# Second expert product of the last seventeen turns as f16 products, and second weights stored as one run per partition

## The reference, cut to what matters

```python
D, HID, E, TOPK = 192, 768, 8, 2
logits = xn2 @ w_gate
top_vals, top_idx = jax.lax.top_k(logits, TOPK)
gates = jax.nn.softmax(top_vals, axis=-1)
gates_full = zeros((T, E)).at[arange(T)[:, None], top_idx].add(gates)
def body(acc, p):
    w1, bb1, w2, bb2, g = p
    h = jax.nn.gelu(xn2 @ w1 + bb1, approximate=False)
    return (acc + g[:, None] * (h @ w2 + bb2), None)
```

## Time and profile before

| what | value |
|---|---|
| profiled execution | 2601.49 us, span 2599.6 us |
| median of three runs | 2596.96 us |
| busy: PE, PEld, DVE | 2382.5, 1836.3, 1658.9 us |
| busy: ACT, POOL | 1158.6, 1042.2 us |
| PE clock granted, mean | 0.935 of full |
| DMA | 262.98 MB, mean 101 GB/s |

### The profile page before, as it was taken

How to read it: one execution, slowest core, us unless ns; L and a number is a source line. 1 busy time by engine, 2 the same in 40 slices (tenths; PEclk the granted TensorE clock), 3 DMA queues, 4 the chain that set the end, 5 groups by cost and what they waited for, 6 DMA issues and landing times. The chain is left out here.

```text
span 2599.6 us, 64053 instructions
## 1 busy us (share of the span) xinstructions
PE 2382.5 (92%) x19496; PEld 1836.3 (71%) x19496; DVE 1658.9 (64%) x4146; ACT 1158.6 (45%) x2240; POOL 1042.2 (40%) x1196
## 2 busy tenths in 40 slices
PE   5589999999999999999999999999999988999886
PEld 4456666666666666677777777777777667888886
DVE  3558888888888888867767776777667731111111
ACT  2234443444433444355555565555555643333332
POOL 2103333333333333244444444444444454555555
PEclk8679999999999998899999999999999999999998
DMA  7432222321223222544344455544534356878774
GB/s 136 150 40 33 33 34 46 45 32 33 34 41 50 32 32 36 135 91 97 102 110 98 106 114 118 113 96 106 117 89 104 95 158 197 219 209 226 203 214 122
DMA packets 250837, 262.98 MB, mean 101 GB/s; under 512 B 35477, under 2 KB 230489, under 8 KB 250777
## 3 DMA queue, kind: packets, MB, share of 16 engines
q1 hardware_dynamic: 213912, 229.95, 37.2%
q0 software_dynamic: 36864, 32.27, 7.2%
HBM read 212.21 MB, written 52.83 MB: 102 GB/s over the span
## 5 line engine op out<-in xcount | busy, mean ns | idle before, releaser
L1347 DVE TENSOR_REDUCE MX<-PS 108x2 f32<-108x648 f32 x576 | 456.0, 824 | 45.6 <-PE PS L1769 40.9
L1042 ACT ACTIVATE pool<-PS 108x648 f32<-108x648 f32 x576 | 387.4, 714 | 216.5 <-PE PS L1792 186.4
L890 POOL DMA_INDIRECT out<-big,tokn x192 | 304.2, 1584 | 436.2 <-DVE big L1497 232.2
L1648 PE MATMUL PS<-WB,big 128*128 128x192 f32 x2304 | 406.3, 332 | 2.5 <-ACT big L1071 2.5
L1071 ACT ACTIVATE big<-PS,WF 128x256 f32<-128x256 f32 x576 | 242.2, 473 | 371.6 <-PE PS L1648 369.9
L1648 PE MATMUL PS<-XE,WF 128*128 128x256 f16 x2880 | 366.4, 279 | 35.3 <-DMA WF<-w1p 28.2
L1648 PEld LDWEIGHTS PS<-WB,big 128*128 128x128 f32 x2304 | 375.6, 192 | 27.4 <-issue 18.5
L1648 PEld LDWEIGHTS PS<-XE,WF 128*128 128x128 f16 x2880 | 277.9, 100 | 91.2 <-issue 33.5
L867 POOL DMA_INDIRECT xbuf<-XR,DST x192 | 190.5, 992 | 242.5 <-issue 197.8
L1497 DVE SCALAR_TENSOR_TENSOR big<-PS,grow,GB 128x192 f32<-128x192 f32 x192 | 71.3, 413 | 273.5 <-POOL GB L878 144.2
L1803 PE MATMUL PS<-pool,Vp 108*32 108x324 f32 x2304 | 217.5, 520 | 0.0
(11 more groups left out here) (197 smaller groups left out, 4104.1 us busy)
## 6 DMA issues: line engine op xcount, KB each, us to landing
WF<-w1p SPq DMA_DIRECT2D x96, 771.5 KB, 5.1
WB<-in_L_ffn_W SPq DMA_DIRECT2D x96, 576.0 KB, 4.7
ximg<-in_x SPq DMA_DIRECT2D x96, 196.0 KB, 5.3
XtR<-xbuf SPq DMA_DIRECT2D x96, 196.0 KB, 2.5
ximg<-in_x SPq DMA_DIRECT2D x96, 195.1 KB, 8.7
B2t<-in_L_ffn_b SPq DMA_DIRECT2D x96, 96.0 KB, 5.3
out<-R SPq DMA_DIRECT2D x32, 243.0 KB
w1p<-WF SPq DMA_DIRECT2D x8, 768.0 KB, 4.0
```

The costliest lines, as they stand in the source:

```text
L890: nc.gpsimd.indirect_dma_start(rows_out, bass.IndirectOffsetOnAxis(ap=tokn[:, i, s_:s_ + 1], axis=0), Yt[:, i, s_, :], None, bounds_check= ...
L1042: nc.scalar.activation(Pr[:, at:at + 2, :], pair(("st", p))[0:TP, :, 0:T], ACT.Exp, scale=SCALE2).then_inc(S["ex"], 1)
L1347: nc.vector.tensor_reduce(MX[:, qt, g, 64 * jj:64 * jj + 64:32], pair(("s", p))[0:TP, :, 0:T], AX.X, ALU.max).then_inc(S["mx"], 1)
L1648: last = nc.tensor.matmul(out_ap, lhsT, rhs, start=(i == 0), stop=(i == len(products) - 1))
```

## The change

1. **Second weights and bias row in one run.** Two DRAM tensors hold, for each expert and partition, 1152 numbers of second weights and 192 of second bias, 5376 bytes in one run. `w2p` holds float32 and is read in the turns up to 14. `w2h` holds the weights times 64, split into f16 high and low halves, and is read in turns 15 to 31 (loads issued in CLOSE and TILES). One DMA in `load_down` takes the place of two.
2. **Filling them.** Before turn 2, SP writes the bias rows of both. In turns 2 and 3, which are now written out instead of being in the loop, four steps `down` each split one expert's second weights on ACT and DVE (128x1152 per instruction), and SP writes them to `w2h`. After turn 3, SP issues 8 DMAs from DRAM to DRAM that fill `w2p`.
3. **Turns of tiles alone.** Gelu writes back in place into PE's accumulator (`ge_alone`, same instructions and shapes). ACT copies each unit to f16 (`gh`, 128x512), DVE subtracts that from the accumulator and writes the rest as f16 (`gl`, 128x512). The second product is 36 f16 products in place of 12 float32 ones (high by high, high by low, low by high). A bank of `W1` is now free when `gl` is done, and `W2` waits for `gl`. `gm` has one more small instruction (gate divided by 64).

```diff
+W2ROW = NC * D + D
...
+DOWN = {2: (0, 1, 2, 3), 3: (4, 5, 6, 7)}
+ALONE = B + 2 - LAG
...
+ALONE_AHEAD = dict(ACT=("ghi",), DVE=("glo", "gr"))
...
-    ("gm", 0), ("gb", 0), ("lr", 0), ("W1", 0, 0), ("ge", 0, 0), ("X", 1), ("xe", 1), ("gm", 1), ("gb", 1), ("lr", 1),
-    ("W1", 0, 1), ("ge", 0, 1), ("W1", 0, 2), ("ge", 0, 2), ("lu", 0), ("W1", 1, 0), ("ge", 1, 0), ("X", 2),
...
+    ("gm", 0), ("gb", 0), ("lr", 0), ("W1", 0, 0), ("ge", 0, 0), ("gh", 0, 0), ("gl", 0, 0), ("X", 1), ("xe", 1),
+    ("gm", 1), ("gb", 1), ("lr", 1), ("W1", 0, 1), ("ge", 0, 1), ("gh", 0, 1), ("gl", 0, 1), ("W1", 0, 2),
+    ("ge", 0, 2), ("gh", 0, 2), ("gl", 0, 2), ("lu", 0), ("W1", 1, 0), ("ge", 1, 0), ("gh", 1, 0), ("gl", 1, 0),
+    ("X", 2), ("xe", 2), ("W1", 1, 1), ("ge", 1, 1), ("gh", 1, 1), ("gl", 1, 1), ("W2", 0, 0), ("W2", 0, 1),
+    ("yv", 0), ("ld", 0), ("ad", 0), ("gm", 2), ("gb", 2), ("lr", 2), ("W1", 1, 2), ("ge", 1, 2), ("gh", 1, 2),
+    ("gl", 1, 2), ("lu", 1), ("W1", 2, 0), ("ge", 2, 0), ("gh", 2, 0), ("gl", 2, 0), ("X", 0), ("xe", 0),
...
+                out.insert(12 + 40 * j, ("down", k))
...
-    name = FREED[step[0]]
+    name = "glo" if step[0] == "W1" and turn.plan is TILES else FREED[step[0]]
...
+        hid16 = big[:, 0:3 * NC * TILE].bitcast(F16).rearrange("p (r s c t) -> p r s c t", r=3, s=2, c=NC)
...
+        def down_views(k):
+
+            w = WF1[:, k % 3, 0:NC * D].bitcast(F16).rearrange("p (s n) -> p s n", s=2)
+            return WB2[:, k % 2, 0:NC * D], w[:, 0, :], w[:, 1, :]
...
+            def down(k):
+                if k < 2:
+                    sp.wait_ge(att_lo, ATT)
+                    sp.wait_ge(stg_lo, NSTG)
+                else:
+                    sp.wait_ge(down_lo, k - 1)
+                sp.dma_start(WB2[:, k % 2, 0:NC * D].rearrange("p (c n) -> p c n", c=NC),
+                             w2[k].rearrange("(c p) n -> p c n", p=128)).then_inc(down_in[k % 2], 16)
+
+            def down_out(k):
+                sp.wait_ge(down_lo, k + 1)
+                sp.dma_start(w2h[k, :, 0:NC * D], WF1[:, k % 3, 0:NC * D]).then_inc(w2h_out[k % 3], 16)
...
+                w2m = w2h if plan[0] is TILES or plan[0] is CLOSE else w2p
...
-                sp.dma_start(WB2[:, i, :, :], w2[bass.ds(e, 1), :, :].rearrange("a (c p) n -> p (a c) n", p=128)
+                sp.dma_start(WB2[:, i, :], w2m[bass.ds(e, 1), :, :].rearrange("a p n -> (a p) n")
                              ).then_inc(S[f"down{i}"], 16)
-                sp.dma_start(B2t[:, i, :], b2[bass.ds(e, 1), :].to_broadcast([128, D])).then_inc(S[f"down{i}"], 16)
...
+            for w in (w2p, w2h):
+                sp.dma_start(w[:, :, NC * D:].rearrange("e p n -> p e n"),
+                             b2.rearrange("(a e) n -> a e n", a=1).to_broadcast([128, E, D])).then_inc(b2_out, 16)
+            for k in range(2):
+                down(k)
+            for b in DOWN:
+                run(Turn(ATTEND, b, b - 1, b - 2, None))
+            for e in range(E):
+                sp.dma_start(w2p[e, :, 0:NC * D].rearrange("p (c n) -> p c n", c=NC), w2[e].rearrange("(c p) n -> p c n", p=128)
+                             ).then_inc(w2_out, 16)
...
+            def down(k):
+                v, hi, lo = down_views(k)
+                act.wait_ge(down_in[k % 2], 16 * (k // 2 + 1))
+                if k < 3:
+                    act.wait_ge(w1_out[k], 16 * len(range(k, E, 3)))
+                else:
+                    act.wait_ge(w2h_out[k % 3], 16 * (k // 3))
+                nc.scalar.activation(hi, v, ACT.Copy, scale=WSC).then_inc(down_hi, 1)
...
+            def ge_alone(m, i, u):
+                act.wait_ge(S["w1"], due("w1", m, 3 * i + u + 1))
+                ps = bank(("W1", i, u))
+                for a in range(2):
+                    c = 2 * u + a
+                    half = ps[:, TILE * a:TILE * a + TILE]
+                    last = nc.scalar.activation(half, half, ACT.Gelu,
+                                                bias=WF1[:, i, 2 * HID + c:2 * HID + c + 1], scale=1.0 / WSC)
+                last.then_inc(S["gelu"], 1)
+
+            def gh(m, i, u):
+                act.wait_ge(S["gelu"], due("gelu", m, 3 * i + u + 1))
+                if u == 0:
+                    act.wait_ge(S["o_full"], due("o_full", m - 1, i + 1))
+                nc.scalar.activation(hid16[:, i, 0, 2 * u:2 * u + 2, :], bank(("W1", i, u)).rearrange("p (a t) -> p a t", a=2),
+                                     ACT.Copy).then_inc(S["ghi"], 1)
...
                 for s_ in range(2):
                     last = nc.vector.scalar_tensor_tensor(Yt[:, i, s_, :], bank(("W2", i, 0))[:, D * s_:D * s_ + D],
-                                                          grow[:, i, s_:s_ + 1], GB[:, i % 2, s_, :], ALU.mult, ALU.add)
+                                                          gates[:, i, s_:s_ + 1], GB[:, i % 2, s_, :], ALU.mult, ALU.add)
                 last.then_inc(S["y_done"], 1)
+
...
+            def gl(m, i, u):
+                dve.wait_ge(S["ghi"], due("ghi", m, 3 * i + u + 1))
+                ps = bank(("W1", i, u)).rearrange("p (a t) -> p a t", a=2)
+                nc.vector.tensor_tensor(hid16[:, i, 1, 2 * u:2 * u + 2, :], ps, hid16[:, i, 0, 2 * u:2 * u + 2, :],
+                                        ALU.subtract).then_inc(S["glo"], 1)
...
+                if plan[0] is TILES:
+                    dve.wait_ge(S["gm"], due("gm", m, i + 1))
+                    nc.vector.tensor_scalar(grs[:, i, :], grow[:, i, :], 1.0 / WSC, None, ALU.mult).then_inc(S["gr"], 1)
...
+                alone = turn.plan is TILES
                 if s_ == 0:
-                    pe.wait_ge(S["gelu"], due("gelu", m, 3 * i + 3))
-                    pe.wait_ge(S[f"down{i}"], due(f"down{i}", m, 32))
+                    split_or_not = "glo" if alone else "gelu"
+                    pe.wait_ge(S[split_or_not], due(split_or_not, m, 3 * i + 3))
+                    pe.wait_ge(S[f"down{i}"], due(f"down{i}", m, 16))
                     free(pe, turn, ("W2", i, 0))
-                last = chain(bank(("W2", i, 0))[:, D * s_:D * s_ + D],
-                             [(hid[:, i, c, 128 * s_:128 * s_ + 128], WB2[:, i, c, :]) for c in range(NC)])
+                r = slice(128 * s_, 128 * s_ + 128)
+                if alone:
+                    products = [(hid16[:, i, k, c, r], WH2[:, i, n, c, :]) for c in range(NC) for k, n in ((0, 0), (0, 1), (1, 0))]
+                else:
+                    products = [(hid[:, i, c, r], WB2[:, i, D * c:D * c + D]) for c in range(NC)]
+                last = chain(bank(("W2", i, 0))[:, D * s_:D * s_ + D], products)
                 if s_ == 1:
                     last.then_inc(S["o_full"], 1)
```

More of the change, by code:

```diff
@@ L1080, in run @@
                         stage(step[1])
+                        continue
+                    if kind == "down":
+                        down(step[1])
                         continue
```

75 lines of the change are left out of this document (57 added, 18 removed), and 7 rows, old and new, of the table TILE_STEPS.

## The result

The changed kernel takes 2656.57 us (median of 4 runs, 2650.69 to 2661.55) against 2595.65 us of the kernel before on the same chip: ratio 1.0239 [1.0208, 1.0269], 61 us more. The forecast was 2611 and its range ended at 2637. The profiled execution took 2653.14 us with a span of 2651.3 us; that of before 2601.49 and 2599.6.

The account below looks back on a forecast made before the run. The prediction took the tile turns as set by a ring of adds, each waiting for the previous landing, with PE close behind. Tile turns +5, turns 2 and 3 +7, copies +2 made 2615 profiled, 2611 as median; range 2584 to 2637.

Parts of the forecast that it names:

- Turns 2 and 3, forecast +7 (0 to 21): Eight `down` steps: +7 us, near two thirds of DVE's 11.4; 0 if DVE's gaps cover them, 21 if all counts.
- Copies, forecast +2 (0 to 15): Eight DRAM-to-DRAM copies after turn 3: +2 us; no cost at 320 GB/s, turn 4 delayed 15 us at 127 GB/s.
- Tile turn, forecast +0.3 us (-1.0 to +1.2): Last 17 turns: changed steps between successive adds sum to +0.3 us a turn, +5 us in all, bounds -17 and +20.
- Layout: forecast -0.9 a turn: Tile turns: longer runs make each second-weight load 0.3 us shorter, 0.9 us a turn, part of it reaching the adds.
- f16: forecast +1.2: Tile turns, terms besides shorter loads: -1.2 from tile 0 to 1, +2.1 to 2.4 for late first weights, +0.2 for clock.
- late first weights: Tile turns, step from tile 1 to 2: `load_up` issued 8 us after tile 0's add delays tile 1's add, +2.1 to 2.4.
- the -1.2 from tile 0 to 1: Tile turns: step from tile 0's add to tile 1's falls from 10.3 to about 9.1 us.
- The chain behind `gm 1`: Tile turns: work from an add's landing to `yv` takes 6.8 us of 9.3; at half clock 9.6, then setting the adds.
- The clock decides: Rival, 20%: PE's longer idles halve its clock every tile turn and the chain behind `gm 1` gates the add: 2626.
- The copies hold turn 4: Rival, 8%: the eight DRAM-to-DRAM copies delay turn 4, 13 us above the forecast: 2624.
- Shorter loads win: Rival, 25%: tile turns' adds land sooner with less ahead in the queues, -17 us, +7 for turns 2 and 3: 2587.
- PE is the bound: Rival, 4%: PE's 92% busy share sets the time, so f16 products save 49 us, +9 elsewhere: 2557.

Follow-up runs that it names:

- Layout alone: Changed kernel's one-run second weights with bias rows, eight copies kept, but no `down` steps and float32 tile turns: 0.9935 of the kernel before; copies spread, 0.9921 and 0.9918.
- Staging with `down` in its place: Changed kernel with `down` steps and copies where they were, but tile turns in float32 with the earlier step list, f16 copy written and unused: 1.0073 of the kernel before.
- both moves: Changed kernel with DVE's half of each `down` 14 places behind ACT's and the eight copies one a turn from turn 4: 1.0116 of the kernel before.
- the fillers: 24 unneeded matmuls per tile turn added to both moves, ahead of `W1 1 1`: 1.0035; with `gm 1` behind `gl 0 2` too, ahead of `W1 2 2`: 0.9995.

## Why the prediction was wrong

Three ratios split the loss. Layout alone: -0.65%, -17 us. Staging with `down` in its place: 1.0073 - 0.9935 = +1.38%, +36 us. f16 products in the tile turns: 1.0239 - 1.0073 = +1.66%, +43 us. That the three add up to the measured +61 follows from how they are made and proves nothing; but the traces give nearly the same for the last part, 27.12 - 24.61 = 2.5 us a turn, 43 us over 17 turns. Against the forecast of +14 the miss is 47 us, of which 27 lie in turns 2 and 3, 12 in the tile turns and 7 in turn 4.

*Turns 2 and 3, forecast +7 (0 to 21): the step that failed.* The durations were right: 1.352 us (at most 1.43) and 1.160 (at most 1.26). The engine time was also near: with `down` moved so that it waits for nothing, turns 2 and 3 take 57.1 + 59.8 us against 52.2 + 55.4 without `down`, +9 us, and some of that is clock too (0.91 and 0.86 for 0.97 and 0.91). That 7 is so close is partly luck, for an idle share of 13% argues for nearer 10 of the 11.4 us. What the sum lacked is the clock. I had taken the idles that follow as a cost of their own length, and weighed half clock only for the tile turns. Here they cost about 25 us more (34 less the 9): PE's matmuls themselves ran at half speed, for 68 of the 141.8 us of turns 2 and 3 against 10 of 107.8 before, and through ACT's queue this came back on `down`. Of the 25 us, 14 are PE's longer busy time (122.3 us against 108.0 with both moves), the rest is waiting. The bound of 21 counted waiting, and a bound on what the waiting does to PE's speed was missing. So was DVE's meeting with POOL, which made an addition 1.53 us longer.

The trace of the kernel before held a warning that I did not read. In its own staging turns, where `stage` splits the first weights on the same two engines, there is a stretch of the same kind, which begins beside the last of these steps (bounds, length, busy as above):

```profile
125.50:159.60 34.10, 29.29 (x171) 16.36 (x171) 12.28 (x27) 11.67 (x22) 5.42 (x9) 0.50 0.43 60
```

The Trainium skill ("TensorE: Matmul & The Clock Gate", What's actually happening) says that for modeling the ramp to full speed costs under 1% of a typical kernel's span. That is said of one ramp, and it would be too low a price for this schedule, in which the clock falls again and again: 25 us in turns 2 and 3 (the waits that grew with it included) and, by the fillers, some 20 in the tile turns are 1.7%.

*Copies, forecast +2 (0 to 15).* By themselves they cost 2 to 4 us, as forecast. In the changed kernel they landed late enough that turn 4 was 8.7 us longer, and with `down` moved, some 16; spread out, turn 4 is back at 53.3. The 8.7 are inside the bound. The way is the one that was named, DVE waiting for the text behind the copies:

```profile
328.00 0.88 DVE L1328 BATCH_NORM_STATS2 st6f<-H 108x6 f32<-108x192 f32 x3 [6.96 <-DMA H<-in_txt]
```

*Tile turn, forecast +0.3 us (-1.0 to +1.2), measured +1.0.* `gh` 597 ns for 0.60 and `gl` 689 ns for 0.68 were right, and so was the place of PE's idle (4.98 us for "some 4") and its half clock (2.31 us for ten products). The parts were off in opposite ways, and that the sum stayed inside its range is partly luck. Layout: forecast -0.9 a turn for three loads, measured -1.5; 1.2 of it without the bias row's DMA, which had no price in my sum. f16: forecast +1.2, measured +2.4 to +2.5. By steps, against the layout alone, f16 adds 0.04, 2.21 and 0.27 us. The 2.21 us from tile 1 to 2 are what the sum has there for late first weights (2.1 to 2.4), though they are issued 5.6 us after tile 0's add and not 8. What failed is the -1.2 from tile 0 to 1. It took the 10.32 us of one turn for the step, where the mean is 9.49, and against that the changed kernel gains 0.06. The chain behind `gm 1` mostly did not hold the add: in the turn shown `yv 0` was done 8.5 us after the landing, and the add at 2357.60 still waited for a landing. But the order of `gm 1` costs 22 us all the same; that it acts by later loads fits their times of issue (5.6, 4.3 and 3.7 us in the changed kernel, with `gm 1` moved, and in the layout alone), and is not shown by a run of its own.

*Rivals.* "The clock decides" (2626) named the right mechanism, and the fillers bear it out; it put it only in the tile turns. "The copies hold turn 4" was right too, with 8.7 us for its 13, and came on top of the others. "Shorter loads win" (2587) was right for the layout alone and wrong for the whole, since f16 used it up. "PE is the bound" is refuted by every f16 kernel here: PE's work shrank and no turn went below the float32 one with the new layout. So the rule of the Trainium skill ("Perfetto Trace Analysis", Identifying the Most-Contended Engine), to optimize the busiest engine first, would have misled here.

*Signs named ahead.* 13 turns at 26.0 to 26.8: 27.1, wrong. PE idle ahead of a `W1` released by `gl`: right. PE busy near 20 us a turn: 22.0, the half clock. POOL still waiting for landings: right. Turns 2 and 3 longer by 3 to 4 us each: 17, wrong. A turn 4 that starts with DVE waiting for the text, named as a sign of being wrong: it came, 6.96 us.

**Left open.** Why an idle of 1.54 us is followed by 34 us at 0.50 with PE busy 91% in them, while one of 1.55 us, from the same cause one turn ahead, is followed by 10.2 us. How much of the loss in turns 2 and 3 comes from the waits for ACT and how much from the meeting with POOL: the moves take both away. And the f16 kernels with less coupling stay 0.8%, 20 us, behind: 9 us are `down`; with all three `gm` later, 25.08 us a turn for 24.34 is 13 us and places the rest; with the fillers it is 5 us, and some 6 are not placed. No kernel with f16 tile turns and without any `down` step was measured.

## What to carry to other kernels

- When work is put into a full schedule, price the wait that it adds ahead of TensorE by what follows at half clock, not by its length. Put the second engine's half so late that it never waits for the first, and look at what the third engine does at that moment.
- Take the steps of a ring as means over many turns; one turn (10.32 us for a mean of 9.49) gave a gain that was not there.
- On an in-order engine, a step that frees a bank must not stand behind a step that waits for a DMA's landing. Fix the order before adding banks.
- Time the parts of a combined change alone: here the layout alone is the best kernel found, 0.992 of the one before, and the f16 products hid it.
